# Retention tail in two halves of the heads, the gate's Silu at the head of the chunk

## The reference

```python
# one layer: x is (1, 16384, 1024)
x = x + retention(layernorm(x))          # H = 16 heads, DK = 64, DV = 128, chunks of C = 64
x = x + moe(layernorm(x))                # 8 experts, top 2, hidden 4096

# retention, per chunk, with the state S carried from chunk to chunk:
o_inter = (qi * dq) @ S
A       = (qi @ ki.T) * Dmat
o_intra = A @ vi
S       = gC * S + (ki * dkv).T @ vi
# then, per head:
rms = o * rsqrt(mean(o * o, axis=-1) + 1e-5) * g_norm_w
out = (rms * (g * sigmoid(g))) @ Wo
```

## Time and profile before

| | |
|---|---|
| median of 3 runs | 7612.3 us (7598.43 to 8332.49) |
| profiled execution | 7620.56 us |
| its span on the slowest core (core 3) | 7619.0 us |
| spans of the 8 cores | 7572.6 to 7619.0 us |
| TensorE busy | 5826.8 us, 76% |
| VectorE busy | 2066.3 us, 27% |
| ScalarE busy | 2211.9 us, 29% |
| GpSimd busy | 208.5 us, 3% |

### The profile page before, as it was taken

The page is one execution under the profiler, slowest core; times in us unless marked ns, Lnnn a source line. Parts: engine busy times, 40 slices in busy tenths (PEclk is TensorE's granted clock), DMA queues, the critical chain, the costliest instruction groups (busy, mean ns, idle before and its releaser), DMA issues.

```text
span 7619.0 us, 78192 instructions; the slowest of 8 cores (7572.6 to 7619.0 us)
## 1 busy us (share of the span) xinstructions
PE 5826.8 (76%) x29760; PEld 2773.8 (36%) x29760; DVE 2066.3 (27%) x2420; ACT 2211.9 (29%) x2970; POOL 208.5 (3%) x111
## 2 busy tenths in 40 slices
PE   2878888788882333333369999999999999999998
PEld 1434334343441222222224444444444444444443
DVE  1434444344442333333311111111111111111111
ACT  4434344344323333333321111211112111121111
POOL 0000000000000000000000000000000000000000
PEclk9999988999995555555579999999999999999999
DMA  7222222221112111111132212212212212112121
GB/s 172 72 92 74 72 86 74 86 79 66 61 37 64 31 31 31 31 31 31 31 49 41 45 23 45 45 23 45 42 25 45 35 32 45 33 34 45 26 42 45
DMA packets 142602, 383.35 MB, mean 50 GB/s; under 512 B 11034, under 2 KB 14874, under 8 KB 138146
## 3 DMA queue, kind: packets, MB, share of 16 engines
q0 software_dynamic: 73888, 151.03, 11.5%
q1 hardware_dynamic: 68354, 227.31, 9.8%
HBM read 487.39 MB, written 41.94 MB: 69 GB/s over the span
## 4 chain that ended last, share of the span: by engine, by line
PE 69%; ACT 10%; issue 8%; DVE 7%; DMA 3%; POOL 2%; ACTq 0%; DVEq 0%; SPq 0%; POOLq 0%
PE f_pX L1125 23%; PE f_pH L1107 23%; PE pP L447 16%; DMA xsw<-x_pref 2%; PE pA L1047 2%; POOL r_o L1026 2%; ACT f_hT L1115 1%; ACT xsw L404 1%; ACT lnxT L441 1%; DVE r_ssq L1010 1%; PE pO L983 1%; PE pKV L573 1%; ACT r_g L1019 1%; ACT r_RT L956 1%; ACT kfS L532 1%
## 5 line engine op out<-in xcount | busy, mean ns | idle before, releaser
L1125 PE MATMUL f_pX<-f_w2q,f_hT 128*128 128x512 bf16 x8192 | 1788.6, 379 | 144.2 <-ACT f_hT L1115 144.2
L1107 PE MATMUL f_pH<-ln2TS,f_w1q 128*128 128x512 bf16 x8192 | 1791.5, 379 | 19.6 <-DMA f_w1q<-w 19.6
L1115 ACT ACTIVATE f_hT<-f_pH,f_b1L 128x512 bf16<-128x512 f32 x1024 | 705.7, 689 | 2978.7 <-PE f_pH L1107 2978.7
L1132 DVE SCALAR_TENSOR_TENSOR accS<-f_pX,WeS,accS 128x1024 f32<-128x1024 f32 x512 | 657.3, 1284 | 3066.1 <-PE f_pX L1125 3066.1
L1125 PEld LDWEIGHTS f_pX<-f_w2q,f_hT 128*128 128x128 bf16 x8192 | 792.3, 98 | 1140.5 <-issue 203.7
L1107 PEld LDWEIGHTS f_pH<-ln2TS,f_w1q 128*128 128x128 bf16 x8192 | 802.1, 98 | 988.7 <-issue 24.3
L447 PE MATMUL pP<-wvS,lnxT 128*128 128x512 bf16 x4096 | 953.4, 392 | 248.9 <-ACT kfS L532 223.5
L447 PEld LDWEIGHTS pP<-wvS,lnxT 128*128 128x128 bf16 x4096 | 403.2, 100 | 793.4 <-issue 385.9
L447 PE MATMUL pP<-wkS,lnxT 128*128 128x512 bf16 x2048 | 484.7, 392 | 0.0
L540 DVE CAST vbf<-pP 128x512 bf16<-128x512 f32 x256 | 177.0, 691 | 1111.5 <-PE pP L447 1111.4
L532 ACT ACTIVATE vbf<-pP 128x512 bf16<-128x512 f32 x256 | 153.1, 598 | 849.6 <-PE pP L447 773.0
(11 more groups left out here) (126 smaller groups left out, 3425.1 us busy)
## 6 DMA issues: line engine op xcount, KB each, us to landing
f_w1q<-w POOLq DMA_DIRECT2D x32, 2048.0 KB, 14.3
f_w2q<-w POOLq DMA_DIRECT2D x32, 2048.0 KB, 14.1
xsw<-x_pref SPq DMA_DIRECT2D x112, 512.0 KB, 4.3
xt<-x_pref SPq DMA_DIRECT2D x112, 512.0 KB, 5.1
g_s<-gf SPq DMA_DIRECT2D x16, 1024.0 KB, 5.9
r_g<-g_s SPq DMA_DIRECT2D x32, 512.0 KB, 5.8
xsw<-x_loc SPq DMA_DIRECT2D x16, 512.0 KB, 3.9
xt<-x_loc SPq DMA_DIRECT2D x16, 512.0 KB, 4.6
```

Source lines behind the costliest of these rows:

```text
L1107: ins = X.matmul(pH[hb][:, :], w1q[wb][:, kt * 1024 + ht * 128: kt * 1024 + (ht + 1) * 128], ln2T[:, kt * TB + tg * 512: kt * TB + (tg + 1 ...
L1115: return X.activation(hT[tgb][:, ht * 512:(ht + 1) * 512], pH[hb][:, :], AF.Gelu, bias=b1L[:, bcol:bcol + 1])
L1125: ins = X.matmul(pX[tb][:, nb_ * 512:(nb_ + 1) * 512], lhs, w2q[wb][:, kt * 1024 + nb_ * 512: kt * 1024 + (nb_ + 1) * 512], start=(kt == 0 ...
L1132: E("vector", lambda X, tau=tau, ex=ex, tb=tb: X.scalar_tensor_tensor(accS[:, tau * D:(tau + 1) * D], pX[tb][:, :], We[:, tau * NE + ex: t ...
```

## The change

- The k tile of 128 tokens gets two buffers instead of one.
- The Silu of g is written at the head of each chunk, after the loads and ahead of the copy of the state.
- Sum of squares, Sqrt, reciprocal, scaling, product, transposes and evacuation are written inside the loop over the halves, each for 8 heads and 1024 columns, after the state's addition of that half. All transposes and evacuations of half 0 are written ahead of the matmuls of half 1.
- The product with g runs on VectorE instead of GpSimd.
- The transposes go to a PSUM tile of their own, `pO3T`, with one bank for each chunk, instead of `pTr`.
- The dependency buffers of `osb`, `osq`, `o4`, `o3T` and `rstt` are split by half.

```diff
-    ktk_one = e(nc.sbuf_tensor("r_k", [128, D], BF16))
-    ktk = [ktk_one, ktk_one]
-    b_ktk_one = Buf()
-    b_ktk = [b_ktk_one, b_ktk_one]
+    ktk = [e(nc.sbuf_tensor(f"r_k{i}", [128, D], BF16)) for i in range(2)]
+    b_ktk = [Buf() for _ in range(2)]
...
+    pO3T = e(nc.psum_tensor("pO3T", [128, 2048], BF16))
+    b_pO3T = [Buf("pO3T0"), Buf("pO3T1")]
...
             ld(grc[0:64, :], g_s[ch * 64:(ch + 1) * 64, :], [b_grc], [b_gs])
+            E("scalar", lambda X: X.activation(grc[0:64, :], grc[0:64, :], AF.Silu),
+              reads=[b_grc], writes=[b_grc])
             E("scalar", lambda X, ci=ci: X.activation(RT[ci][64:128, :], Sf[64:128, :], AF.Identity),
...
                 E("vector", lambda X, cols=cols: X.tensor_add(Sf[64:128, cols],
                                                               Sf[64:128, cols], pO[64:128, 0:1024]),
                   reads=[b_Sf, b_pOkv], writes=[b_Sf])
-
-            sq_cols = ssq[:, ci * H:(ci + 1) * H]
-            E("vector", lambda X, sq=sq_cols: X.tensor_reduce(
-                sq[0:64, :], osq[0:64, :].rearrange("p (h v) -> p h v", h=H), AX.X, ALU.add),
-              reads=[b_osq], writes=[b_rstt[ci]])
-            rc = rstt[:, ci * 32:ci * 32 + H]
-            E("scalar", lambda X, sq=sq_cols, rc=rc: X.activation(
-                rc[0:64, :], sq[0:64, :], AF.Sqrt, bias=cst[0:64, 0:1], scale=cst[0:64, 1:2]),
-              reads=[b_rstt[ci], b_cst], writes=[b_rstt[ci]])
-            E("vector", lambda X, rc=rc: X.reciprocal(rc[0:64, :], rc[0:64, :]),
-              reads=[b_rstt[ci]], writes=[b_rstt[ci]])
-            E("scalar", lambda X: X.activation(grc[0:64, :], grc[0:64, :], AF.Silu),
-              reads=[b_grc], writes=[b_grc])
...
-            E("gpsimd", lambda X, ci=ci: X.tensor_tensor(o4[ci][0:64, :], osb[0:64, :],
-                                                         grc[0:64, :], ALU.mult),
-              reads=[b_osb, b_grc], writes=[b_o4[ci]])
...
+                sq = ssq[:, ci * H + hh * 8: ci * H + (hh + 1) * 8]
+                rc = rstt[:, ci * 32 + hh * 8: ci * 32 + (hh + 1) * 8]
+                E("vector", lambda X, sq=sq, cols=cols: X.tensor_reduce(
+                    sq[0:64, :], osq[0:64, cols].rearrange("p (h v) -> p h v", h=8),
+                    AX.X, ALU.add),
+                  reads=[b_osq[hh]], writes=[b_rstt[ci][hh]])
+                E("scalar", lambda X, sq=sq, rc=rc: X.activation(
+                    rc[0:64, :], sq[0:64, :], AF.Sqrt, bias=cst[0:64, 0:1], scale=cst[0:64, 1:2]),
+                  reads=[b_rstt[ci][hh], b_cst], writes=[b_rstt[ci][hh]])
+                E("vector", lambda X, rc=rc: X.reciprocal(rc[0:64, :], rc[0:64, :]),
+                  reads=[b_rstt[ci][hh]], writes=[b_rstt[ci][hh]])
+                def f(X, rc=rc, cols=cols):
+                    o3 = osb[0:64, cols].rearrange("p (h v) -> p h v", h=8)
+                    r3 = rc[0:64, :].unsqueeze(2).broadcast_to((64, 8, DV))
+                    return X.tensor_tensor(o3, o3, r3, ALU.mult)
+                E("vector", f, reads=[b_osb[hh], b_rstt[ci][hh]], writes=[b_osb[hh]])
+                E("vector", lambda X, ci=ci, cols=cols: X.tensor_tensor(
+                    o4[ci][0:64, cols], osb[0:64, cols], grc[0:64, cols], ALU.mult),
+                  reads=[b_osb[hh], b_grc], writes=[b_o4h[hh]])
+                def f(X, ci=ci, hh=hh):
+                    for b in range(8):
+                        ins = X.transpose(pO3T[:, ci * 1024 + (hh * 8 + b) * 64:
+                                               ci * 1024 + (hh * 8 + b + 1) * 64],
+                                          o4[ci][0:64, hh * 1024 + b * 128:
+                                                 hh * 1024 + (b + 1) * 128],
+                                          ident[0:64, 0:64])
+                    return ins
+                E("tensor", f, reads=[b_o4h[hh], b_ident], writes=[b_pO3T[ci]])
...
+                E("scalar", f, reads=[b_pO3T[ci]], writes=[b_o3T[ci * 2 + hh]])
...
-        E("tensor", f, reads=[b_o3T, b_wo], writes=[b_pA])
+        E("tensor", f, reads=b_o3T + [b_wo], writes=[b_pA])
```

More of the change, by code:

```diff
@@ L719, in _retention @@
     b_RT = [Buf() for _ in range(2)]
-    osb = e(nc.sbuf_tensor("r_o", [128, H * DV], F32)); b_osb = Buf()
-    osq = e(nc.sbuf_tensor("r_osq", [128, H * DV], F32)); b_osq = Buf()
+    osb = e(nc.sbuf_tensor("r_o", [128, H * DV], F32)); b_osb = [Buf(), Buf()]
+    osq = e(nc.sbuf_tensor("r_osq", [128, H * DV], F32)); b_osq = [Buf(), Buf()]
     o4_one = e(nc.sbuf_tensor("r_o4", [128, H * DV], BF16))
     o4 = [o4_one, o4_one]
-    b_o4_one = Buf()
-    b_o4 = [b_o4_one, b_o4_one]
-    o3T = e(nc.sbuf_tensor("r_o3T", [128, 16 * 128], BF16)); b_o3T = Buf()
+    b_o4h = [Buf(), Buf()]
+    o3T = e(nc.sbuf_tensor("r_o3T", [128, 16 * 128], BF16))
+    b_o3T = [Buf() for _ in range(4)]
     rstt = e(nc.sbuf_tensor("r_rst", [128, 64], F32))
-    b_rstt = [Buf() for _ in range(2)]
+    b_rstt = [[Buf(), Buf()], [Buf(), Buf()]]
     ssq = e(nc.sbuf_tensor("r_ssq", [128, 2 * H], F32))
@@ L826, in p2_router @@
                                X.activation(osq[:, 1024:2048], xa, AF.Identity, accum_out=sm))[-1],
-          reads=[b_accT[tau]], writes=[b_osq, b_stats2[buf]])
+          reads=[b_accT[tau]], writes=b_osq + [b_stats2[buf]])
         E("vector", lambda X: (X.tensor_scalar_mul(mean, sm, 1.0 / D),
@@ L991, in _retention @@
                                                               AF.Identity),
-                  reads=[b_pOo], writes=[b_osb])
+                  reads=[b_pOo], writes=[b_osb[hh]])
                 E("scalar", lambda X, cols=cols: X.activation(osq[0:64, cols], pO[0:64, 0:1024],
                                                               AF.Square),
-                  reads=[b_pOo], writes=[b_osq])
+                  reads=[b_pOo], writes=[b_osq[hh]])
                 def f(X, ci=ci, hs=hs):
@@ L1025, in _retention @@
-            E("vector", f, reads=[b_osb, b_rstt[ci]], writes=[b_osb])
-            E("gpsimd", lambda X, ci=ci: X.tensor_tensor(o4[ci][0:64, :], osb[0:64, :],
-                                                         grc[0:64, :], ALU.mult),
-              reads=[b_osb, b_grc], writes=[b_o4[ci]])
[L1029 to L1040, removed]
+                sq = ssq[:, ci * H + hh * 8: ci * H + (hh + 1) * 8]
+                rc = rstt[:, ci * 32 + hh * 8: ci * 32 + (hh + 1) * 8]
@@ new lines, in _retention, with f @@
+                E("tensor", f, reads=[b_o4h[hh], b_ident], writes=[b_pO3T[ci]])
+                def f(X, ci=ci, hh=hh):
+                    dst = o3T[:, :].rearrange("p (b t) -> p b t", b=16)
+                    src = pO3T[:, ci * 1024 + hh * 512: ci * 1024 + (hh + 1) * 512]                         .rearrange("p (b t) -> p b t", b=8)
+                    return X.activation(dst[:, hh * 8:(hh + 1) * 8, ci * 64:(ci + 1) * 64],
+                                        src, AF.Identity)
+                E("scalar", f, reads=[b_pO3T[ci]], writes=[b_o3T[ci * 2 + hh]])
```

## The result

The changed kernel takes 1.2% longer: the ratio to the kernel before is 1.0122 (95% interval 1.0102 to 1.0142). Single executions stand at 7692.9, 7694.9, 7697.8 and 7693.7 us against 7596.3, 7598.4 and 7612.3.

What follows compares the result with a forecast made beforehand. A serial chain of waits in retention, no engine, bounds the kernel; 3.21 + 5.16 - 1.43 - 1.30 = +5.64 us a tile, 16 times, plus 1.30 for the last router, gives +91.5 us: 7704 us, range 7650 to 7770.

Steps and rivals of the forecast that it cites:

- Queues in written order: Retention halves: half 1's output matmuls wait behind half 0's transposes, so nothing overlaps; second output matmul 10.07 us after first.
- Tail of chunk 1: Chunk 1, first output matmul to output projection: projection starts at 19.80 us instead of 21.23, a gain of 1.43 us.
- DVE product: Product with g on VectorE, per half: taken as 1.22 us, upper bound 2.24, which would add 65 us in all.
- Silu in chunk 0: Head of chunk 0, ahead of the state's copy: Silu and its table load lengthen the path by 3.21 us.
- Chunk 1's copy: State's copy starting chunk 1: Silu ahead of it waits for the load of g, so it comes 5.16 us later.
- Router: Router's Sqrt (L835): no table load now that Sqrt is the last table; gain 1.30 us in 15 of 16 routers.
- Rival B: Chunk 1: the load of g is hidden, copy +1.85 us instead of +5.16; 7651 us in all; chance 0.07.
- rival C: Chunk 1: the exposed load of g takes 10.0 us, 85 us on top, 7789 us; chance 0.07.
- Rival A: Retention: halves overlap and Silu fills ScalarE's idle time; -9.8 us a tile, -156 in all, 7456 us; chance 0.06.
- Rival D: Output projection: runs at the lower clock throughout, 14.4 us instead of 9.37; 81 us on top, 7785 us; chance 0.03.
- Rival E: ScalarE: a table switch costs more than its row, 1.38 us, with one fewer a tile; 7682 us; chance 0.05.
- Costed at nothing: Second k buffer, separate PSUM tile for transposes and buffers split by half: claimed to change the time by nothing.

Runs made afterwards that it cites:

- e3: The changed kernel without the halves: all 16 heads at once, Silu still ahead of the state's copy, product on VectorE; 7661 us.
- e5: The kernel before with Silu moved behind the state's copy and the product on VectorE, all heads at once; 7527 us.
- e9: Changed kernel with Silu behind state's copy, both halves' output matmuls before all transposes, g product before norm, one Sqrt with preloaded table; 7331 and 7337 us.
- e1: The changed kernel with two lines swapped, Silu of g behind the copy of the state; ratio 0.9901 to the kernel before.
- e2: The changed kernel with Silu writing its own bf16 tile, squares in bf16; cores 0 to 3 span 7607 to 7631 us, against 7669 to 7681.
- e6: The kernel before with only Silu moved, behind the copy of the state; product on GpSimd, all heads at once; 7566 and 7598 us.
- e10: Repeat run: the kernel before with Silu behind the state's copy and product on VectorE, all heads at once; 7508 us.
- e4: The kernel before with only Silu moved ahead of the state's copy; product on GpSimd, all heads at once; ratio 1.0143.

## Where the prediction failed, and what of it was right

**The step that failed is the base of the sum.** The prediction set its +91.5 us on 7612.3, the median of three executions of the kernel before, one of which took 8332 us, and its range of 7650 to 7770 is built from terms of the chain alone. The median of the changed kernel's 9 executions is 7858 us, outside the range: 5 of the 9 took 7858 us or more. No step of the chain did that, since the kernel before has the same: the median of 10 of its executions is 7915, 303 us above the base. So the metric holds a spread between executions of one kernel that is three times the change, and the sum put it at nothing, with the 8332 in view. Where this spread comes from was not tried.

**The chain was right.** By the ratio the kernel is 1.2% slower, as forecast, and the four executions named above lie 6 to 11 us under the 7704. That they lie so near is in part luck. The tiles of the two traces give 5.1 x 16 = 82 us (80.5 by the windows of the stage) where 91.5 were summed, and the two profiled executions are 72.3 us apart (7620.56 and 7692.88); the means of the executions, 7694.8 and 7602.3, are 92.5 apart. Executions of the kernel before differ by 32 us (7596 to 7628), so the last 10 us of the agreement show nothing. Term by term, as means over tiles 1 to 15:

- **Queues in written order.** Right. The second output matmul comes at 9.93 us (said: 10.07), and e3 and e5 show that the halves in this order cost 2.1 us up to the product, e9 that the same matmuls start at 3.36 once nothing stands before them.
- **Tail of chunk 1, -1.43.** Measured -1.40 up to the projection (19.87 instead of 21.27, mean of 15 tiles). The projection itself took 0.14 less, not foreseen.
- **DVE product at 1.22.** Measured 1.217 for all 64. The upper bound from GpSimd's row wasn't needed.
- **Silu in chunk 0, +3.21.** Measured +3.17. The load stands in each of the 32 chunks, so Sigmoid's table doesn't serve Silu here: these are the table loads of retention at Silu (`L956`) and at the norm's Sqrt (`L1016`), by line.

```profile
L956 ACT ACT_TABLE_LOAD x32 | 41.1, 1283 | 52.5 <-DMA r_g<-g_s 52.2
L1016 ACT ACT_TABLE_LOAD x32 | 41.1, 1283 | 51.3 <-DVE r_ssq L1012 51.3
```

- **Chunk 1's copy, +5.16.** Measured +5.00. Rival B (the load of g is hidden) and rival C (it takes 10 us) both fall by the 3.3 us that ScalarE waits.
- **Router, -1.30.** Measured -1.52. The missing load gives 1.3; 0.2 more lies elsewhere in the router and isn't explained. S is as short in the other kernels with halves (15.72 in e1, 15.78 in e2, 15.59 in e9), and 15.84 to 15.96 in those written from the kernel before (e3 to e6, e10).
- **Sum, +5.64 a tile.** Measured +5.1. Of the 0.54 between them 0.33 are the router and the projection, the rest the two terms of Silu.
- **Rival A** (halves overlap, Silu in idle time) falls for the changed kernel. e9 has the overlap that it describes, reached by another order, and is faster than its price of 7456: it also has one Sqrt for all heads, with its table loaded ahead, and the product with g under that Sqrt. How the difference divides among these wasn't measured.
- **Rival D** falls: the projection takes 9.2 us on average, no more than before (9.3).
- **Rival E** falls: a table load costs 1.30 from its start to the function's, here as in the earlier trace rows.
- **Costed at nothing:** the second k tile, `pO3T` and the split buffers. No run takes them out alone. e3 has none of them, and its P, Q and R fit what the halves alone were expected to cost.

## What to carry to other kernels

In this kernel splitting the chain in two gained only once the second half's instructions stood ahead of the first half's waiting ones in every queue. So read the order as written, engine by engine, before counting any overlap. Put an operation that needs a load into an engine's idle stretch behind the work that the path needs, not ahead of it; two swapped operations were worth 2% here. And before an operation is moved out of a chain, look at what it hides: 3.2 us of Silu gave only 0.4 a chunk in e6, since a scaling of 2.28 us had lain under it.

## What was not expected of the hardware

The output projection, 32 equal matmuls, takes between 8.5 and 10.0 us up to its addition, from tile to tile of the same execution of the changed kernel (8.96 to 9.52 before). It starts at a granted clock of 0.5 and ends at 1.0 (1.2 and 2.4 GHz), and the moment at which the clock rises differs: in the tile whose matmuls start at 3096.92 and take 8.48 us it is 0.52 over the first 2.98 us and 1.00 from there on; in the one at 3198.17, which take 9.04, it is 0.50 over the first 2.83 us, 0.80 over the next 3.00 and 1.00 after that. What sets that moment wasn't tried. Also, an operation on GpSimd began 0.33 us after the VectorE operation that it waited for (e4: 3156.33 to 3156.66), while VectorE needed 0.11 to follow itself and TensorE 0.14 to follow GpSimd.
